# Attention over 32 heads: q's high and low parts loaded into 64 partitions and doubled by GpSimd, k's rows of a head stored high rows first

## The reference, cut to what matters

```python
Q = jnp.einsum('btd,hkd->bthk', x, W_Q) + b_Q
K = jnp.einsum('btd,hkd->bthk', x, W_K) + b_K
scores = jnp.einsum('bqhk,bshk->bhqs', Q, K) / jnp.sqrt(64)
attn = jax.nn.softmax(scores, axis=-1)
out_h = jnp.einsum('bhqs,bshk->bqhk', attn, V)
return jnp.einsum('bqhk,hdk->bqd', out_h, W_O) + b_O
```

## Time and profile before

| | before |
|---|---|
| time, median of 3 runs | 3157.94 us |
| profiled execution: span, first to last instruction | 3342.4 us |
| attention in it, from the first score matmul (964.9 us) to the end | 2377.5 us |
| PE busy | 3124.5 us (93%) |
| DVE busy | 2625.2 us (79%) |
| POOL busy | 2101.7 us (63%) |
| ACT busy | 1965.3 us (59%) |
| DMA, queue q1 | 71.1% of 16 engines |

### The profile page before, as it was taken

The page is one execution under the profiler, slowest core; times in us unless marked ns, Lnnn a source line. Parts: engine busy times, 40 slices in busy tenths (PEclk is TensorE's granted clock), DMA queues, the critical chain, the costliest instruction groups (busy, mean ns, idle before and its releaser), DMA issues.

```text
span 3342.4 us, 53910 instructions
## 1 busy us (share of the span) xinstructions
PE 3124.5 (93%) x13443; PEld 1609.9 (48%) x13444; DVE 2625.2 (79%) x2773; ACT 1965.3 (59%) x3797; POOL 2101.7 (63%) x2148
## 2 busy tenths in 40 slices
PE   7965659999979999999999999999999999999998
PEld 3433323445544555555555555455555555555554
DVE  8600013433359999999999999999999999999995
ACT  4500003203447777777777777677777777777775
POOL 4877771001126777777777777667777777777776
PEclk9987769999989999999999999999999999999999
DMA  8810017776658988879899888898888889888987
GB/s 315 326 66 23 17 42 283 252 178 209 229 155 227 227 226 215 220 202 222 225 223 225 215 217 204 210 253 221 225 220 217 214 209 221 225 223 218 219 204 182
DMA packets 318996, 685.52 MB, mean 205 GB/s; under 512 B 120749, under 2 KB 170680, under 8 KB 318544
## 3 DMA queue, kind: packets, MB, share of 16 engines
q1 hardware_dynamic: 289744, 626.48, 71.1%
q0 software_dynamic: 29184, 58.22, 5.4%
HBM read 198.37 MB, written 159.51 MB: 107 GB/s over the span
## 4 chain that ended last, share of the span: by engine, by line
PE 64%; DMA 2%; SPq 1%; DVE 1%; issue 1%; POOL 1%; ACT 0%; POOLq 0%; ACTq 0%
PE at_ps L1110 26%; PE at_ps L1142 25%; PE at_ps L1157 8%; PE at_ps L1123 5%; DMA at_moved<-at_blocks 1%; SPq L934 1%; DVE at_half_max L1239 1%; DVE at_blocks L1256 1%; DMA out<-ahead_acc 0%; POOL at_moved L1052 0%; POOL ahead_acc L1067 0%; ACT at_prob L1193 0%; DMA ahead_acc<-base 0%; SPq L783 0%; POOL ahead_acc L1044 0%
## 5 line engine op out<-in xcount | busy, mean ns | idle before, releaser
L1193 ACT ACTIVATE at_prob<-at_ps,at_neg_max 128x1024 f32<-128x1024 f32 x1024 | 1150.4, 1123 | 323.7 <-DVE at_neg_max L1244 284.5
L1239 DVE TENSOR_REDUCE at_half_max<-at_ps 128x1 f32<-128x1024 f32 x1024 | 1202.2, 1215 | 26.6 <-PE at_ps L1110 25.2
L1256 DVE STREAM_TRANSPOSE at_blocks<-at_prob 128x1792 f32<-128x1792 f32 x512 | 1043.1, 2037 | 5.9 <-DMA at_moved<-at_blocks 3.2
L1052 POOL COPY at_moved<-at_blocks 32x1792 f32<-32x1792 f32 x512 | 858.2, 1676 | 159.2 <-DVE at_blocks L1256 61.0
L1110 PE MATMUL at_ps<-ahead_k_hl,ahead_q_hh 128*128 128x512 f32 x2048 | 854.1, 417 | 22.9 <-ACT at_prob L1193 16.2
L1142 PE MATMUL at_ps<-at_moved,at_v 128*64 128x512 f32 x3584 | 863.2, 595 | 6.9 <-DMA at_moved<-at_blocks 6.9
L1110 PE MATMUL at_ps<-ahead_k_hl,ahead_q_ll 128*128 128x512 f32 x2048 | 809.4, 395 | 0.0
L1067 POOL TENSOR_TENSOR ahead_acc<-ahead_acc,at_scaled 128x256 f32<-128x256 f32 x512 | 376.5, 735 | 228.0 <-ACT at_scaled L1205 105.6
L1110 PEld LDWEIGHTS at_ps<-ahead_k_hl,ahead_q_hh 128*128 128x128 f32 x2048 | 388.6, 190 | 96.9 <-ACT at_prob L1193 24.2
L1142 PEld LDWEIGHTS at_ps<-at_moved,at_v 128*64 128x64 f32 x3584 | 262.5, 138 | 354.5 <-issue 299.6
L1205 ACT ACTIVATE at_scaled<-at_ps,at_inv 128x256 f32<-128x256 f32 x512 | 242.9, 474 | 316.2 <-PE at_ps L1157 263.0
(11 more groups left out here) (112 smaller groups left out, 2783.7 us busy)
## 6 DMA issues: line engine op xcount, KB each, us to landing
at_moved<-at_blocks SPq DMA_DIRECT2D x1536, 224.0 KB
ahead_k_hl<-k_parts SPq DMA_DIRECT2D x64, 512.0 KB, 8.2
ahead_q_hh<-q_parts SPq DMA_DIRECT2D x128, 256.0 KB, 4.3
ahead_q_ll<-q_parts SPq DMA_DIRECT2D x128, 256.0 KB, 6.1
xbuf<-pr_zeros SPq DMA_DIRECT2D x32, 512.0 KB, 3.9
q_parts<-pr_part_hi SPq DMA_DIRECT2D x64, 256.0 KB
q_parts<-pr_part_lo SPq DMA_DIRECT2D x64, 256.0 KB
k_parts<-pr_part_hi SPq DMA_DIRECT2D x64, 256.0 KB
```

Source lines behind the costliest of these rows:

```text
L1052: nc.gpsimd.tensor_copy(moved[r * 32:(r + 1) * 32, parity, r, :, :, :], blocks[r * 32:(r + 1) * 32, parity, r, :, :, :]).then_inc(diag_don ...
L1193: nc.scalar.activation(prob[:, i % 2, half * 1024:(half + 1) * 1024], ps[:, banks[0]:banks[1], :].rearrange("p b c -> p (b c)"), ACT.Exp, ...
L1239: nc.vector.tensor_reduce(half_max[:, i % 2, half:half + 1], ps[:, banks[0]:banks[1], :], AX.XY, ALU.max).then_inc(max_step, 1)
L1256: nc.vector.transpose(blocks[:, parity, :, j, :, :].rearrange("p c t k -> p t c k"), prob[:, (s["s"] - 1) % 2, 0:MOVED * P].rearrange("p ( ...
```

## The change

- `store_qk`: a unit of k (two heads, 128 rows) is stored by four DMAs of 64 rows and not by two of 128, so that a head's 128 rows in HBM are 64 high rows and then 64 low rows. The counts that others wait for follow (`STORES`).
- `load_q`: each part is loaded once, 64 rows into partitions 0 to 63.
- `double_q` on POOL, new: it waits for `q_loaded`, copies partitions 0 to 63 of `q_hh` and of `q_ll` to partitions 64 to 127, and waits for both copies (`q_doubled`). It is called once at the start, and then at the head of slots 3, 7, 11 and 15, for the group that begins in the next slot.
- `score` on PE waits for `q_doubled` in place of `q_loaded`.

```diff
--- before.py
+++ after.py
@@ -171,6 +171,7 @@
         ROUTED = 3
         ZEROS_FIRST = 10
         COUNTS_AT = 7
+        STORES = (32, 64)
         EXPERTS_AT = 24
 
         def qk_units(c):
@@ -205,11 +206,17 @@
 
             def store_qk(c):
                 for n, u, is_key, pair in qk_units(c):
-                    dst = scr["k"].rearrange("(x a) t -> a x t", a=2) if is_key else scr["q"]
                     wait_apart(sp, qk_lo, n + 1, sp_waits)
                     for part, src in ((0, part_hi), (1, part_lo)):
-                        sp.dma_start(dst[part, pair * P:(pair + 1) * P, bass.ds(c * CH, CH)],
-                                     src[:, u % 4, :].bitcast(F32)).then_inc(qk_stored[u % 4], 16)
+                        if is_key:
+                            for h in range(2):
+                                row = (2 * pair + h) * P + part * DH
+                                sp.dma_start(scr["k"][row:row + DH, bass.ds(c * CH, CH)],
+                                             src[h * DH:(h + 1) * DH, u % 4, :].bitcast(F32)
+                                             ).then_inc(qk_stored[u % 4], 16)
+                        else:
+                            sp.dma_start(scr["q"][part, pair * P:(pair + 1) * P, bass.ds(c * CH, CH)],
+                                         src[:, u % 4, :].bitcast(F32)).then_inc(qk_stored[u % 4], 16)
 
                     if isinstance(n, int) and n % 2 and ZEROS_FIRST + n // 2 < ZR:
                         zero_rows(ZEROS_FIRST + n // 2)
@@ -235,7 +242,7 @@
                                  ).then_inc(v_stored[n % 4], 16)
 
             for n in range(4):
-                sp.wait_ge(qk_stored[n], NC * H // 4 * 32)
+                sp.wait_ge(qk_stored[n], NC * H // 4 * STORES[n % 2])
             for n in range(4):
                 sp.wait_ge(v_stored[n], 2 * NT // 4 * 16)
             sp.wait_ge(base_stored, NC * 16)
@@ -321,7 +328,7 @@
                 for n, u, is_key, pair in qk_units(c):
                     bias = (bk if is_key else bq)[:, pair:pair + 1]
                     act.wait_ge(qk_ready, n + 1)
-                    wait_pos(act, qk_stored[u % 4], (c * 4 + u // 4) * 32)
+                    wait_pos(act, qk_stored[u % 4], (c * 4 + u // 4) * STORES[is_key])
                     nc.scalar.activation(part_hi[:, u % 4, :], ps[:, 4 + u % 4, :], ACT.Identity, bias=bias
                                          ).then_inc(qk_hi, 1)
                     if isinstance(c, int):
@@ -460,7 +467,7 @@
                                                    op1=ALU.subtract).then_inc(qk_lo, 1)
 
             for u in range(4):
-                dve.wait_ge(qk_stored[u], NC * H // 4 * 32)
+                dve.wait_ge(qk_stored[u], NC * H // 4 * STORES[u % 2])
             for n in range(2 * NT):
                 dve.wait_ge(v_ready, n + 1)
                 wait_pos(dve, v_stored[n % 4], (n // 4) * 16)
@@ -780,8 +787,7 @@
 
     for part, dst in ((0, start["q_hh"]), (1, start["q_ll"])):
         src = scr["q"][part, bass.ds(h * DH, DH), b * T + g * CH:b * T + (g + 1) * CH]
-        sp.dma_start(dst[:, g % 2, :].bitcast(F32), src.unsqueeze(1).to_broadcast([DH, 2, CH])
-                     ).then_inc(start["q_loaded"][g % 2], 16)
+        sp.dma_start(dst[0:DH, g % 2, :].bitcast(F32), src).then_inc(start["q_loaded"][g % 2], 16)
 
 
 def load_k(sp, scr, start, b, h, side, part):
@@ -822,6 +828,7 @@
 
         v_loaded = m.sems("v_loaded", GT)
         wo_loaded = m.sems("wo_loaded", 2)
+        q_doubled = m.sem("q_doubled")
         early_scored = m.sem("early_scored")
         late_scored = m.sem("late_scored")
         max_step = m.sem("max_step")
@@ -1053,8 +1060,20 @@
                                           blocks[r * 32:(r + 1) * 32, parity, r, :, :, :]).then_inc(diag_done, 1)
                 wait_apart(pool, diag_done, QD * group + 2 * half + 2, pool_waits)
 
+            def double_q(head, g):
+
+                wait_apart(pool, q_loaded[g % 2], 32 * (head * 2 + g // 2) + 32, pool_waits)
+                for q in (q_hh, q_ll):
+                    nc.gpsimd.tensor_copy(q[DH:P, g % 2, :], q[0:DH, g % 2, :].bitcast(F32)).then_inc(q_doubled, 1)
+                wait_apart(pool, q_doubled, 2 * (head * GROUPS + g) + 2, pool_waits)
+
             def body(b, h, s):
                 i = s["s"]
+                if i == 0 and b == 0 and isinstance(h, int) and h == 0:
+                    double_q(0, 0)
+                if i < TILES and i % GT == GT - 1 and not (b == B - 1 and isinstance(h, int) and h == H - 1 and i == TILES - 1):
+                    last = i // GT == GROUPS - 1
+                    double_q(s["head"] + last, (i // GT + 1) % GROUPS)
                 if i == 0 and isinstance(h, tuple):
                     for q in range(GROUPS):
                         pool.wait_ge(base_loaded[q], 16 * (b + 1))
@@ -1096,7 +1115,7 @@
                 g, j, side = i // GT, i % GT, s["side"]
                 if half == 0:
                     if j == 0:
-                        pe.wait_ge(q_loaded[g % 2], 32 * (head * 2 + g // 2) + 32)
+                        pe.wait_ge(q_doubled, 2 * (head * GROUPS + g) + 2)
                     if i == 0:
                         pe.wait_ge(k_loaded[side], 32 * s["pair"] + 32)
                     wait_pos(pe, early_exp, tile - 1)
```

## The result

| | before | after |
|---|---|---|
| time, median of 4 runs each | 3158.06 us | 3902.47 us |
| lowest and highest | 3156.80, 3158.32 | 3896.21, 3905.95 |
| ratio, 95% interval | | 1.235 (1.233 to 1.237) |
| profiled execution, span | 3342.4 us | 3904.3 us |

The change costs 744 us. The forecast was 3985 us, range 3680 to 4250. Four lines of the page of after: the first gives the busy time of each engine, the others are groups of instructions (busy us, mean ns | idle us just before them, and what ended most of it).

The account below looks back on a forecast made before the run. PE was taken to bound attention, 72.57 us a head. Ring 589, clock 205 and 12 for the rest made 806 us on the 3342 us span; scaled to run time, a point between 3920 and 4072: 3985 us, range 3680 to 4250.

Parts of the forecast that it names:

- POOL is late although it is idle: Attention: POOL, busy 378.8 of 511.5 us, begins slots 3, 7, 11, 15 2.91 to 5.40 us after PE begins the next slots.
- ring: Attention: PE and POOL wait for each other each group; a head takes 91.6 us against 72.57, 589 us in all.
- full POOL without the ring: Rival, chance 0.04: in attention only POOL's load counts, 5.6 us a head, 174 us in all, time 3325 us.
- Its rival, 4220 us: Rival, chance 0.13: POOL's casts are as slow as its fp32r subtraction, 232 us more, time 4220 us.
- The stops: PE idle before the scores of slots 8, 12, 0 and 4, waiting for POOL's casts: 6.1, 6.1, 1.6, 5.3 us.
- The clock: PE's clock falls behind three longer stops a head, 2.2 us lost each, 6.6 a head, 205 us in all.
- The stores of k: SP issues six DMAs instead of four for a pair of units, ahead of attention: 5 us, bound 25.
- From profile to time: Profiled span to run time, 184 us apart: shrink everything by 0.945 (3920 us) or only PE's matmuls; 3985 taken between.
- The 4072 us for the other end: Time if all 184 us lie in PE's many short matmuls; a head then shrinks from 98.2 to 95.9 us.
- the range's lower end: Ring without clock loss, casts at the copy's price: 3342 + 589 - 32 + 12, by 0.945, about 3695, rounded down to 3680.
- start and turn of the batch: First doubling delays the first scores by 2 us; PE waits behind POOL in batch 2's first head, 5 us, bounds 0 and 15.
- q's loads: Halving the reads of q relieves nothing, with -7 us as bound.

Follow-up runs that it names:

- e2: After with the casts a slot earlier, at the head of POOL's slots 2, 6, 10 and 14: 3372.76 us, 1.068.
- e3: After with the same casts on ACT instead of POOL, k stored as in after: 3204.70 us, 1.016.
- e8: After without doubling on POOL: q doubled by two DMAs of 64 rows for each part, k stored as in after: 3205.27 us, 1.015.
- e4: After with PE kept busy in its stops by 16, 18 and 18 overwritten matmuls at slots 4, 8 and 12: 3754.32 us, 1.190.
- e0: The kernel before, unchanged, profiled a second time: 3157.28 us, span 3155.7 us.
- e9: e3 with k's weight columns reordered so that each part of a unit of k is stored by one DMA, 64 outermost: 3159.22 us, 1.0004 against before.
- e1: After without casts on POOL: each part of q loaded twice by one DMA with the two copies outermost: 4276.04 us, 1.354.
- e7: e1 with k also stored by one DMA for each part, the pair's two heads outermost: 4773.26 us, 1.511.

## Why the prediction was right, and where it wasn't

- **POOL is late although it is idle.** Right. It rested on the places of both engines in time, not on the busy share. e2 and e3 bear it out: the same casts at another place, or on another engine, and no ring. e8, without casts, gives the base. The price of a full POOL without the ring was about right too: e2 less the 47 us of the stores is 3326 us, and that rival had 3325 (its 174 us not scaled down would give 3332).
- **The ring's parts.** POOL's way from the add of slot 5 to the doubling was put at 14.71 us and took 14.70. The cast was put at 0.70 us, between copy (0.62) and fp32r subtraction (1.63); the row below says 0.606 (ns min/median/max). Its rival, 4220 us, is out. The casts with the release of PE were put at 1.6 us and took 1.21, or 1.33 by the group behind slot 0 (23.13 - 7.88 - 13.92). The 0.2 us in them for the way to PE's first matmul, for which no row was given, were 0.05 (from the second cast's end at 1601.22 to 1601.27).

```profile
L1067 POOL CAST ahead_q_hh<-ahead_q_hh x128: 604/606/609, 829.7 to 3845.0; 64x512 fp32r<-64x512 f32 x128
```

- **The stops.** Forecast 6.1, 6.1, 1.6, 5.3 us in front of slots 8, 12, 0 and 4; measured 5.49, 5.47, 1.35, 4.75. The quicker casts and release explain about half of the difference; the rest is that PE's own work in a group took some 0.2 us more (23.13 - 4.75 = 18.38 behind slot 0, for 18.14).
- **The clock.** The mechanism was right and the size too large: 6.6 us a head against 5.14 (e4 against after). It stood on two stops of before. The head's granted clock was put near 0.85 and was 0.93; DVE is at 72.42 of 95.56 us, 76%, as said.
- **The stores of k.** This term failed: 5 us with a bound of 25, measured 47 (e8, e3) to 50 (first score matmul at 830.9, not 780.8; the other runs with these stores have it at 824 to 831). The step took 0.52 us for each DMA from the earlier trace rows, whatever its rows. SP's queue in e0 and then in after:

```profile
402.88 0.33 SPq L211 DMA_DIRECT2D q_parts<-pr_part_hi  x1
...
404.60 0.33 SPq L211 DMA_DIRECT2D k_parts<-pr_part_hi  x1
405.11 0.33 SPq L211 DMA_DIRECT2D k_parts<-pr_part_lo  x1
406.31 0.33 SPq L211 DMA_DIRECT2D q_parts<-pr_part_hi  x1
```

```profile
404.16 0.35 SPq L218 DMA_DIRECT2D q_parts<-pr_part_hi  x1
404.70 0.33 SPq L218 DMA_DIRECT2D q_parts<-pr_part_lo  x1
405.27 1.18 SPq L214 DMA_DIRECT2D k_parts<-pr_part_hi  x2
406.63 1.13 SPq L214 DMA_DIRECT2D k_parts<-pr_part_lo  x2
408.00 0.39 SPq L218 DMA_DIRECT2D q_parts<-pr_part_hi  x1
```

  A pair of 64-row DMAs holds the queue 1.13 to 1.18 us where one of 128 rows held it 0.33. SP has no pause left, and the period of two units goes from 3.43 to 3.84 us. ACT then waits for the stores of k, and does not in e0 (us in total, times, longest):

```profile
ACT pr_part_hi L332 <- DMA k_parts<-pr_part_lo: 76.7, 57, 3.6
```

  By DVE's first and last low part, the 40 looped pairs took 158.1 us instead of 135.3 (+23). The unlooped units made the first scatter of rows to `xbuf` 17 us later (166.2, not 149.2). Of the other 10 us, the way from the looped pairs to v's projection takes 2.6 more (6.9 for 4.3), that projection 2.3 more, and some 5 were not placed.
- **From profile to time.** This step was wrong, and so was the reading that recording stretches the execution. It spread the 184 us over the whole execution, and PE, or all of it, was to shrink. e0 shows them in one stage ahead of attention, and attention as long as in the first profile. Without the step the sum is 3158 + 806 = 3964 us; the step moved the time 21 us the wrong way. The 4072 us for the other end had a head of 95.9 us, near the 95.56 measured, but by a shrinking that doesn't exist, so that was luck. In the range's lower end, 32 us stand for the copy's price of the casts, where the forecast's own figures give 124 x 2 x 0.08 = 20.
- **The sum in runs.** e8 less before 47 (stores), e4 less e8 549 (ring at full clock), after less e4 148 (clock): 744. Forecast 5, 596 with start and turn of the batch, and 205. The ring (by 47) and the clock (by 57) were too high and the stores (by 42) too low, so the sum was 62 us too high, and the last step added 21: 3985 for 3902. Part of its nearness is thus luck. The 7 us for start and turn of the batch do not show: e4's head is 17.85 us above that of before, which for 31 heads is 553 us, already more than the 549.
- **q's loads** give nothing, as forecast (e9).

## What to carry to other kernels

Before you give an in-order engine that looks partly idle work for which the bounding engine will wait, compare in the timeline how far both have come at that point: POOL's 63% busy meant no slack, and ACT, 59% busy, took the same casts for nothing. Lateness once built into a ring is paid in every round, and again in the clock. If a profile's span is above the runs, find the stage before scaling anything by it, and when a DMA is cut in two, price the issuing queue by DMAs of the new shape.

## What was not expected of the hardware

- **A shorter stop can cost the same.** With stops of 4.18 to 5.01 us instead of 4.75 to 5.49 the lost clock rose from 5.14 to 7.30 us a head, and the head stayed at 95.56 us. Stops of 1.35 us cost nothing. What decides how much a longer stop costs, beside its length, was not settled.
- **A DMA with 2 outermost** burdens other DMAs of its queue as well: k's loads 22.6 us in place of 7.4 (e1), SP's queue 4.6 us for each low store (e7).
- **Half the rows, more issue time:** a store of k held SP's queue 0.47 us at least for 64 rows (after), 0.33 for 128 (e0).
- **A stage ahead of attention took 184 us longer in one profiled execution**, in waits for something outside the core's records; none of the other 12 profiles here shows such a wait.
